# The place of the value product and of the max tiles among the score tiles of an attention kernel

## What is computed

```python
x = x + 0.5 * ffn(layernorm(x))          # shared matrix, one expert matrix, gate of 7 logits, bias
x = x + attention(layernorm(x))
x = x + 0.5 * ffn(layernorm(x))

# attention: 16 heads of 16 features, causal
scores = q @ k.T / 4, masked above the diagonal
out = softmax(scores) @ v, then the output projection
```

## Time and profile before

| | |
|---|---|
| runs | 1315.37, 1317.42, 1318.98 us; median 1317.42 us |
| the profiled execution | 1315.5 us, of which the span of the core's instructions is 1313.7 us |
| granted PE clock, mean over the span | 0.971 of full speed |
| busy over the span | PE 94%, DVE 84%, ACT 70%, POOL 33% |
| one group of stage B in the middle of the run | 24.46 us, of which PE 24.12, DVE 23.10, ACT 19.73, POOL 6.37 us busy |

### The profile page before, as it was taken

One profiled execution on the slowest core, in us unless ns is written; L12 is line 12 of the kernel. 1 busy time (PEld: TensorE's weight loads), 2 busy tenths in 40 slices (PEclk: granted clock), 3 DMA queues, 4 the chain that ended last, 5 costly groups with the idle time before them and its releaser, 6 DMA issues. The chain is left out here.

```text
span 1313.7 us, 36528 instructions
## 1 busy us (share of the span) xinstructions
PE 1232.8 (94%) x9331; PEld 830.1 (63%) x9331; DVE 1105.7 (84%) x3904; ACT 920.8 (70%) x1858; POOL 434.4 (33%) x843
## 2 busy tenths in 40 slices
PE   3999999997999999999999999999999996799996
PEld 3988888875555555555555555555555552699996
DVE  4788888877999999999999999999999994467775
ACT  3666666640787887888888888887888887356664
POOL 3433333301222322322322322322322222577772
PEclk9999999997899999999999999999999999799998
DMA  3366665793464664664664654654654753556651
GB/s 116 129 224 224 224 224 222 241 264 102 77 112 83 101 109 82 104 105 82 109 100 82 109 101 86 109 97 90 109 93 94 105 92 112 189 171 198 197 161 65
DMA packets 121853, 173.74 MB, mean 132 GB/s; under 512 B 44012, under 2 KB 71788, under 8 KB 121804
## 3 DMA queue, kind: packets, MB, share of 16 engines
q1 hardware_dynamic: 121816, 173.30, 56.2%
HBM read 96.08 MB, written 76.02 MB: 131 GB/s over the span
## 5 line engine op out<-in xcount | busy, mean ns | idle before, releaser
L441 DVE CUSTOM_DVE_ANT_0 junk<-banks,mask 128x768 bf16<-128x768 f32 (+7 forms) x1036 | 727.0, 753 | 5.4 <-issue 5.3
L1085 ACT ACTIVATE b_probs<-banks 128x512 f32<-128x512 f32 x1152 | 597.7, 610 | 133.4 <-PE banks L1190 129.4
L1209 PE MATMUL banks<-b_probs,b_vx 128*32 128x512 f32 (+3 forms) x3072 | 308.2, 496 | 4.3 <-POOL b_probs L1045 2.0
L1190 PE MATMUL banks<-qs,ks 50*128 50x512 f32 (+3 forms) x1056 | 308.3, 390 | 0.8 <-ACT b_probs L1085 0.4
L434 PE MATMUL banks<-ks,qs 48*128 48x512 f32 (+3 forms) x1056 | 281.8, 388 | 14.4 <-DVE pm L441 11.1
L434 PEld LDWEIGHTS banks<-ks,qs 48*128 48x128 f32 x1056 | 170.9, 190 | 153.7 <-DVE pm L441 125.5
L166 POOL TENSOR_TENSOR hold_pool<-zero 128x1 f32<-128x1 f32 x192 | 37.0, 193 | 587.3 <-ACT b_probs L1085 444.8
L1190 PEld LDWEIGHTS banks<-qs,ks 50*128 50x128 f32 x1056 | 166.7, 187 | 27.1 <-ACT b_probs L1085 20.8
L1045 POOL TENSOR_SCALAR_AFFINE_SELECT b_probs<-b_probs 128x512 f32<-128x512 f32 x256 | 158.3, 636 | 0.0
L1190 PE MATMUL banks<-b_qs,b_ks 50*128 50x512 f32 (+2 forms) x480 | 142.7, 387 | 0.2
L1209 PEld LDWEIGHTS banks<-b_probs,b_vx 128*32 128x32 f32 x3072 | 70.7, 108 | 109.1 <-issue 80.6
(11 more groups left out here) (118 smaller groups left out, 1941.6 us busy)
## 6 DMA issues: line engine op xcount, KB each, us to landing
scr_qk<-a_qk SPq DMA_DIRECT2D x64, 512.0 KB, 3.0
qs<-scr_qk SPq DMA_DIRECT2D x132, 128.0 KB, 4.5
ks<-scr_qk SPq DMA_DIRECT2D x132, 128.0 KB, 5.1
scr_o<-b_o SPq DMA_DIRECT2D x64, 256.0 KB, 3.5
b_qs<-scr_qk SPq DMA_DIRECT2D x66, 128.0 KB, 3.9
b_ks<-scr_qk SPq DMA_DIRECT2D x66, 128.0 KB, 4.4
a_x<-x SPq DMA_DIRECT2D x16, 512.0 KB, 3.4
scr_x<-a_x SPq DMA_DIRECT2D x16, 512.0 KB, 2.7
```

The source lines that it names most:

```text
L441: ins = dve.tensor_tensor_reduce(self.junk[:, u % 2, off:off + w], pair[:, off:off + w], self.mask[:, 2 * BANK - w:2 * BANK], 1.0, 0.0, AL ...
L1085: act.activation(probs[:, PROB_BUF[s], h, :], score_bank(g, t, last)[:], ACT.Exp).then_inc(p_ready, 1)
L1190: done = pe.matmul(score_bank(g, t, last)[:, off:off + w], ks[g.buf][head_rows(h, SROWS_M), h // 2, j * P:(j + 1) * P], qs[g.buf][head_row ...
L1209: last = pe.matmul(o_bank[2 * D * h:2 * D * (h + 1), col:col + w], vx[g.buf][:, j, h, :], probs[:, PROB_BUF[src], h, off:off + w], start=( ...
```

## The change

The order of the heads becomes 1, 3, 0, 2. The event moves from behind score tile n = 2 to behind n = 1. For n = 3 the max tile comes behind the score tile and not ahead of it. The max tiles run 12 ahead of the score tiles and no longer 13, and the prologue issues one fewer. The transpose stays behind score tile n = 2 of slot 6, where the value product no longer is.

```diff
--- before.py
+++ after.py
@@ -53,7 +53,7 @@
 PAIRS = GH // 2
 
 
-S_ORDER = (1, 0, 2, 3)
+S_ORDER = (1, 3, 0, 2)
 NBUF = 3
 AHEAD = 3
 MASKED = -1.0e38
@@ -1221,7 +1221,7 @@
             def step(g, last):
                 def maxima(s, n):
                     if not last:
-                        t = (s + AHEAD) * GH + n + 1
+                        t = (s + AHEAD) * GH + n
                         if t < TILES:
                             max_tile(g.next(1), t)
                         else:
@@ -1229,16 +1229,19 @@
 
                 for s in range(NSLOT):
                     for n in range(GH):
-                        maxima(s, n)
+                        if n < GH - 1:
+                            maxima(s, n)
                         score_tile(g, s, n, last)
-                        if n == GH - 2:
+                        if n == GH - 1:
+                            maxima(s, n)
+                        if n == 1:
                             event(g, s)
-                            if s == TURN_SLOT and not last:
-                                turn_m(g.next(1))
+                        if n == GH - 2 and s == TURN_SLOT and not last:
+                            turn_m(g.next(1))
 
             for t in range(2 * UNITS_IN_A, TILES):
                 max_tile(Group(0, 0), t)
-            for t in range(AHEAD * GH + 1):
+            for t in range(AHEAD * GH):
                 max_tile(Group(0, 1), t)
                 if t == GH - 1:
                     turn_m(Group(0, 0))
```

## The result

The changed kernel took 1352.82 us (median of four runs, 1347.7 to 1357.2) against 1317.12 us before (1315.37 to 1318.98). The ratio is 1.0277, with a 95% interval from 1.0261 to 1.0294: slower, by 35.7 us. The profiled execution took 1347.7 us with a span of 1345.9.

The account below looks back on a forecast made before the run. Bound by a 2.64 us loop per slot (score tile, exponential, last score tile, value product), DVE close behind. Late transpose 0.84 plus late DVE 0.18 is 1.02 us a group, 31.6 over 31 groups: 1349 us, 2.4% slower, range 1328 to 1363.

Parts of the forecast that it names:

- Ordinary slots stay at 2.64: Stage B: the loop of score tile, exponential, last score tile and value product stays at 2.64 us a slot.
- The transpose is late by DVE's chain behind V5: Unit 17 falls behind V5; transpose at 4.00 us after V5's end, PE standing still 1.0; V6 to V7 +0.84 a group.
- Transpose to V7 1.37: After the late transpose, V7 follows between 1.26 and 1.5 us later, taken as 1.37, against 1.90 before.
- DVE late behind V7, +0.18: Slot V7 to V8: tile 45 waits for DVE's late units, V8 at 4.19 after the transpose against 4.00; +0.18 us.
- The copy of the result, 0: Two slots of nine: copy behind tile a's exponential moves the wait from ACT to PE; 0, bounds -0.15 and +0.05 a group.
- The pair order, 0: Pairs in second place, score tile now ahead of max tile: taken as 0, with +0.3 us a group kept for the range.
- The sum: Stage B: 0.84 + 0.18 = 1.02 us a group, over 31 groups 31.6 us.
- The rival that the transpose isn't late: DVE has the maxima ready in time at the transpose: 8 us less, 1309 us; chance 7%.
- The rival that the stall is given back: DVE and ACT catch up within the group, leaving some 0.4 us a group: 12 us, 1329 us; chance 9%.
- The rival of the clock: PE idling 1 us a group lowers its clock, three slots a group at half clock: 118 us, 1467 us; chance 4%.
- The drain on a change of mode: At the transpose, no longer sharing V6's mode change: another 0.09 us a group, hidden where DVE delays the transpose.

Follow-up runs that it names:

- x2: Changed kernel with max tiles 14 ahead in place of 12 and heads ordered 0, 2, 1, 3; 1316.88 us, ratio 0.9987 against the kernel before.
- x1: Changed kernel with both of DVE's part instructions (L1118, L1120) ahead of unit 0; 1324.86 us, ratio 1.0058 against the kernel before.
- y1: Kernel before with both of DVE's part instructions (L1118, L1120) ahead of unit 0; 1317.84 us, ratio 1.0009.
- y4: Kernel before with both copies of the result one exponential later, behind tile a's exponential; 1313.91 us, ratio 0.9978.
- x4: Kernel before with the pair order alone changed: for n = 0 the max tile comes behind the score tile; 1316.72 us, ratio 0.9995.
- x3: Kernel before with the event alone moved from behind score tile n = 2 to behind n = 1, max tiles still 13 ahead; 1601.14 us, ratio 1.2136.
- z3: Kernel before with max tiles 12 ahead in place of 13 and the changed kernel's head order, event still behind n = 2; 1585.17 us, one run.

## Why the prediction was right, point by point

- **Ordinary slots stay at 2.64.** Right: 2.64 to 2.65 in V8 to V1 and V2 to V4 of every whole-unit kernel.
- **The transpose is late by DVE's chain behind V5.** Right in its mechanism: x2 takes unit 17 ahead of V5 and the loss is gone, x1 takes 1.23 us out of the chain and most of it is gone, y1 shows that this isn't the edit's own gain. The parts: unit 17 read 0.97 after V5's end (0.94 forecast), L1118 at 2.42 (2.38), the transpose at 4.24 (4.00), PE idle 1.11 (1.0). What was mis-sized is the step from L1118 to the transpose: 1.82 us, not the 1.62 of the earlier trace rows. Unit 0 starts 0.28 behind L1118 and the transpose 0.31 behind L1120; at the start of stage B it was 0.15 and 0.24 (320.96 and 322.19 there). Why these gaps differ was not tried.
- **Transpose to V7 1.37.** It was 1.18. ACT's copy did allow slot 7's n = 1 where forecast (matmul at 627.21, 0.84 behind the transpose), and V7 came only 0.34 behind that. The working had mixed two starts: the 0.83 was that of the tile's matmul, but the 0.43 to the value product runs from the load of its weights, which is at 627.13, 0.76 behind the transpose. 0.76 + 0.42 is the 1.18 that was measured, below the 1.26 that I had given as the least. This error and that of the chain nearly cancel, which is luck: V6 to V7 3.79 for 3.74.
- **DVE late behind V7, +0.18.** It was +0.30, but not because DVE was later than forecast: V8 came 4.12 behind the transpose, where 4.19 was forecast, and V7 had come 0.19 too early. DVE's idle time was 1.09 rather than 0.9, and the tile held was 44, by the first read of unit 2, not 45 by the last.
- **The copy of the result, 0.** V1 to V2 fell by 0.08 and V4 to V5 rose by 0.06. The copy started 0.49 behind the start of tile a's exponential (612.26 and 611.77) and V2 came 0.06 behind its end; I had let it start 0.52 behind (a quarter of the 2.07 for four) and taken 0.12 for the semaphore. Single exponentials take 0.60 and start every 0.49; so the loop's 1.21 stands, but it is made of 1.17 for the end of the first exponential and 0.04 behind it, not of 1.09 and 0.12. y4 has this part alone: -0.07 a group.
- **The pair order, 0.** Right by x4; the +0.3 kept for the range wasn't needed.
- **The sum.** 1.02 us a group forecast, 1.11 to 1.13 measured. From the first transpose to the last, over 31 groups, the trace has 794.7 us (317.9 to 1112.6) against 759.3 (322.4 to 1081.7): 35.4 us, 1.14 a group. The 31.6 us forecast for the kernel was 35.7, and 1352.8 came for 1349. That the profiled execution took 1347.7 us, where the working had 1347.1, is luck: its first transpose came 4.5 us earlier than in the kernel before, ahead of anything that the change touches, and the median of the runs lies 5.1 above it, not 1.9.
- **The rival that the transpose isn't late** was laid aside rightly, but its price was wrong: x2 makes it come true (with max tiles further ahead and another order of heads) and gives 1316.9, not 1309: a group of 24.43 for 24.20. I had V7 at 0.42 + 0.83 + 0.11 + 0.43 behind V6's end; ACT's copy started 0.64 behind the transpose, as it stood behind tile a's exponential. The gain put down to the copy, 0.15, is 0.07 by y4.
- **The rival that the stall is given back**: it grows instead in the next slot, V7 to V8 2.94 for 2.64.
- **The rival of the clock**: clock 1.00 throughout the changed kernel's groups. In x3 PE pauses for 0.6 to 1.0 us in every slot and the clock goes from 1.00 to 0.50; in the changed kernel a group of 25.6 us has one pause of 1.11 us and two of some 0.35. The Trainium skill's section on a second failure mode (TensorE: Matmul & The Clock Gate), against which I had set the rows of the last group, tells of a clock that swings between its two levels because PE idles briefly and often between groups of matmuls; x3 and z3 agree with it.
- **The drain on a change of mode** (the Trainium skill, TensorEngine Tiling, Key Properties): in x2 the transpose starts 0.43 behind a score tile where neighbours are 0.34 apart, so the trace agrees with it and with the 0.09 taken; in the changed kernel it is covered by the wait. No run changes the mode alone, so that the 0.09 is the drain is not shown.

## What to carry to other kernels

Before a step is moved in a hand-written order, look for what must be complete on its far side. Here a unit of work for DVE slipped behind a value product of 1.4 us, and the product of that unit was needed three steps on; the margin in the trace had been 0.28 us. When two streams are interleaved, keep the items that are consumed together on one side of a long step, and count banks of a ring when another user takes a turn in it: both cost more than the instructions that were moved.

## What the runs showed of the hardware that I had not expected

- A closed loop of small waits can cost the clock where a single longer wait doesn't. In x3, with pauses of 0.6 to 1.0 us in each slot, the granted clock fell to 0.50 for some 13 us in nearly every group (1601 us in all), though PE was busy all through much of that time; in the changed kernel a pause of 1.11 us a group left it at 1.00. In x3's first groups (350.0 to 408.7) the clock stood at 1.00 too, though PE was busy for only 22.9 and 23.0 us of each. What decides when it falls, no run here shows.
- ACT starts the next instruction before the one before it is over: exponentials of 0.60 us start every 0.49 (four take 2.06), and the copy behind one started after 0.49 too. An estimate that lets them queue end to end is 0.1 too long for each; one that divides the time of four by four lets the first end 0.08 too early.
